# Two of three matmuls for the 64 rest rows in three down products, and five statistics in step 4

## The chip, the cores and the metric

The kernel runs on one core of a Trainium2 chip. The metric is the time of one execution on the device, in microseconds (us). Before the change three runs gave 2494.76 us as the median (2494.2 to 2495.37). A profile was taken of one further execution of the same kernel.

## The reference, cut to what matters

With x of shape [4, 1024, 1024] (batch, channel, length), the block computes

```
xn   = layernorm(x)                                   # over the last axis
s    = xn + attention over the 4 batches at each position (softmax of 4x4 scores)
gate = xn @ Wg.T ; up = xn @ Wu.T                     # Wg, Wu: 2752 x 1024, NF4 codes times scales
y    = (silu(gate) * up) @ Wd.T                       # Wd: 1024 x 2752
out  = x + s * silu(y)
```

The 2752 inner rows are 21 tiles of 128 and a rest of 64. That rest is what one half of the change is about.

## The kernel before, in words

**Numbers.** All large products run on TensorE in float16 with float32 accumulation. Each float32 operand is split in two parts, high (`hi`, the value rounded to float16) and low (`lo`, what is left). A product takes three matmuls for each 128 rows: hi·hi, hi·lo and lo·hi (`TERMS`, line 1715). The 2x2 blocks of each matrix product go through Strassen-Winograd sums, so that there are seven products instead of eight; they are called p1 to p7, and `OPERAND` gives the operand index (0 to 6) of each.

**Steps.** The gate and up products take 88 steps: two halves h of the tokens, and in each 44 pairs (u, j) of a weight tile u (0 to 21) and a token group j. In step s TensorE does four products of step s and three of step s-1, each of 12 matmuls of 128x512. VectorE (DVE) adds the results up (L1536, L1543, L1548 for p6, p7, p5; L1568, L1570 for p4, p3), multiplies gate by up (L1573, L1526), and in the same steps prepares the weights of later steps and the operands of the down products. ScalarE (ACT) decodes the NF4 codes (eight `Prelu` passes, L770), rounds to float16 (L783, L932), and applies silu (L980 on p2's sum, L990 on the other). TensorE may start p7 of step s only when VectorE has done L1568 of step s-2 (`free_bank`, semaphore `c21_made`), and p1 of step s only when ScalarE has done L980 of step s-2 (`silA_made`).

**Order on an engine.** It is written by hand. VectorE's side work of a step is put into six slots, 0 to 5, by tables (`background`, line 1470): slot 0 before L1536, 1 before L1543, 2 before L1548, 3 and 4 after it, 5 behind L1573 of the step. `STAT_AT` is such a table: it says in which step and slot the layernorm statistics (L1234, `stats`, two `bn_stats` of 128x512) of token tiles 16 to 31 are taken. Tiles 16 and up have two buffers between them, so SyncE (SP) loads tile t+2 from `in_x` (L522, `load_stat`) only when the statistics of tile t are done. SP is in order too: at step s it issues first what the step stores (L590, seven stores where the step has a job) and the scales (L566), then the loads of that step's table row. From step 8 on the statistics are used (`roots`, L1222 to L1229), and tiles 16 to 31 are normalised and transposed.

**Down products.** They come last: 28 rounds i, seven products (order p1, p6, p2, p7, p5, p4, p3) for each of four token groups tp. A round has four groups g of 11 x 3 = 33 matmuls (L1932), one group for each 128 output rows. Its operands, 2816 KB of weights from `wdsc` and 2816 KB of activations from `isc`, come by DMA into a ring of two (`load_ring`, L840 and L841, issued by ACT at the beginning of the round before). Both scratch tensors are filled from `stage` slots by `store_stage`. Row block k = 10 holds the rest: in operands 1, 2 and 3 only its partitions 64 to 127 come from real rows, since the other half is zero in both parts. After a round's group VectorE, ScalarE and GpSimd (POOL, L739) finish an output tile, and SP stores it (L703).

Of the kernel before, what the change touches and what calls it, by code (L numbers as in the profile page):

```python
# [15 lines left out]
P = 128  # L16
# [27 lines left out]
DOWN_ORDER = ["p1", "p6", "p2", "p7", "p5", "p4", "p3"]  # L44
OPERAND = {"p1": 0, "p2": 1, "p3": 2, "p4": 3, "p5": 4, "p6": 5, "p7": 6}
# [28 lines left out]
def step_of(h, u, j):  # L74
# [3 lines left out]

SPARE = [s for s in range(4, 40) if PASS[s][0] % 2]

STAT_AT = {3: {0: 16, 3: 17}, 4: {0: 18, 3: 19, 5: 20}, 5: {5: 21}, 6: {0: 22, 1: 23, 2: 24, 3: 25, 5: 26},
           7: {0: 27, 1: 28, 2: 29, 3: 30, 5: 31}}
ROOTS_AT = 8
NORM_AT = {8 + 2 * i: (16 + 2 * i, 17 + 2 * i) for i in range(8)}
XJOB_AT = {s: (2 + i // 4, i % 4) for i, s in enumerate([s for s in SPARE if s >= 24][-8:])}
# [61 lines left out]
NDOWN = 11  # L147
# [3 lines left out]
for _d in range(NDOWN):  # L151
    for _i in range(3):
        DOWN_AT[NSTEP + 3 * _d + _i] = (_d, _i)
        if _d + 1 < NDOWN:
            RAMP_AT[NSTEP + 3 * _d + _i] = (NU + _d + 1, [0, 2, 5][_i], [2, 5, 8][_i])
DOWN_OPS = [[0, 4], [5, 1, 3], [6, 2]]


STAGED = {}
# [12 lines left out]
STAGE_AT, SLOT, SLOT_USE = [], [], []  # L172
# [9 lines left out]
def slot_uses(k, last):  # L182

    return SLOT[:last + 1].count(k)
# [57 lines left out]
def build(nc, x, xt, gu_codes, d_codes, scales, out):  # L242
# [4 lines left out]
    RR = I - FT * P  # L247
    GB = H // QB
    DB = I // QB
    CH = 512  # L250
    assert RR == QB and NB == 4 and KT == 8 and FT == 21 and C == 1024

    isc = nc.dram_tensor("isc", [4, 7, P, NDOWN, 2, CH], F16, kind="Internal").ap()
    wdsc = nc.dram_tensor("wdsc", [7, P, NDOWN, 2, CH], F16, kind="Internal").ap()
# [8 lines left out]
    with ExitStack() as ctx:  # L263
# [3 lines left out]
        def sem(name):  # L267
            return ctx.enter_context(nc.semaphore(name))
# [30 lines left out]
        stage = [carve(kb, 2, F16).rearrange("p (s t) -> p s t", s=2) for kb in (210, 212, 214, 216, 168, 170, 176, 178, 180, 182)]  # L299
# [14 lines left out]
        ring_i = [carve(56 * b, 22, F16).rearrange("p (k s t) -> p k s t", k=NDOWN, s=2) for b in (0, 1)]  # L314
        ring_w = [carve(56 * b + 22, 22, F16).rearrange("p (k s g m) -> p k s g m", k=NDOWN, s=2, g=4) for b in (0, 1)]
        ring_if = [carve(56 * b, 22, F16) for b in (0, 1)]
# [31 lines left out]
        ps = ctx.enter_context(nc.psum_tensor("ps", [P, 8, 512], F32))  # L348
# [31 lines left out]
        st_out = [sem(f"st_out{i}") for i in range(NALL)]  # L380
# [7 lines left out]
        w_in = [[sem(f"w_in{b}{i}") for i in (0, 1)] for b in (0, 1)]  # L388
        xb_in = [[sem(f"xb_in{j}{o}") for o in range(7)] for j in (0, 1)]
        w4_in = sem("w4_in")  # L390
        prod = sem("prod")
        p1_copied = sem("p1_copied")
        silA_made = sem("silA_made")
# [16 lines left out]
        ri_in = [sem("ri_in0"), sem("ri_in1")]  # L410
# [94 lines left out]
        def _(sp):  # L505
# [75 lines left out]

            def store_stage(c, o):
                n = STAGED[c + (o,)]
                if c[0] == "d":
                    sp.wait_ge(d_lo, c[1] * 7 + D_ORDER.index(o) + 1)
                    dst = wdsc[o, :, c[1], :, :]
                else:
                    sp.wait_ge(c_lo, lo_count(c, o))
                    dst = isc[c[2], o, :, c[1], :, :] if c[0] == "i" else xsc[c[1] - 2, o, :, c[2], :, :]
                sp.dma_start(dst, stage[SLOT[n]]).then_inc(st_out[SLOT[n]], 16)  # L590


            sp.dma_start(s_all, scales).then_inc(scales_in, 16)
# [7 lines left out]
            for a, b in ((0, 8), (8, 16), (16, 22)):  # L601
                n = (b - a) * GB
                sp.dma_start(gsc[a:b, :, :].rearrange("t b m -> (t b) m"), st_g[0:n, a * 16:a * 16 + P]).then_inc(sc_out, 16)
            sp.wait_ge(sct_evac, 4)
            for a, b in ((0, 8), (8, 16), (16, 21)):
                n = (b - a) * GB
# [24 lines left out]
            for s in range(TOTAL):  # L631
# [31 lines left out]
                if s in DOWN_AT:  # L663
                    d, i = DOWN_AT[s]
                    for o in DOWN_OPS[i]:
                        store_stage(("d", d), o)
# [20 lines left out]
            def load_xn(tp, kt):  # L687
                n = tp * KT + kt
                if n >= 2:
                    sp.wait_ge(ms_step, 8 * (n - 1))  # L690
                else:

                    sp.wait_ge(prod, len(PRODS))
                sp.dma_start(xn_r[n % 2], xnsc[tp // 2, kt, :, :, :]).then_inc(xn_in[n % 2], 16)

            def load_xr(tp, kt, a, n):
# [8 lines left out]
            for i in range(28):  # L705
                tp, r = i // 7, i % 7
                if i and (i - 1) % 7 in (2, 4, 5, 6):
                    n, kt, a = tile_no(i - 1, 3)
# [4 lines left out]
                if r in (2, 4, 5, 6):  # L713
                    for g in range(4):
                        n, kt, a = tile_no(i, g)
                        load_xr(tp, kt, a, n)
                    for g in range(3):
                        n, kt, a = tile_no(i, g)
                        store_out(tp, kt, a, n)
            n, kt, a = tile_no(27, 3)  # L720
# [21 lines left out]
        def _(act):  # L742
# [82 lines left out]
            def load_ring(i):  # L825
                tp, r = i // 7, i % 7
                o = OPERAND[DOWN_ORDER[r]]
                b = i % 2
                if i >= 2:
                    act.wait_ge(prod2, 4 * (i - 1))  # L830
                last = max(STAGED["i", p, tp, o] for p in range(NDOWN))
                for k in range(NALL):
                    if slot_uses(k, last):
                        act.wait_ge(st_out[k], 16 * slot_uses(k, last))
                if i < 7:
                    last = max(STAGED["d", d, o] for d in range(NDOWN))
                    for k in range(NALL):
                        if slot_uses(k, last):
                            act.wait_ge(st_out[k], 16 * slot_uses(k, last))
                act.dma_start(ring_wf[b], wdsc[o, :, :, :, :].rearrange("p k s c -> p (k s c)")).then_inc(rw_in[b], 16)  # L840
                act.dma_start(ring_if[b], isc[tp, o, :, :, :, :].rearrange("p k s c -> p (k s c)")).then_inc(ri_in[b], 16)  # L841

            def reloads(s, part):

# [242 lines left out]
            for s in range(2, TOTAL + 1):  # L1087
# [76 lines left out]
                if s in GRAM_AT:  # L1164
                    k = GRAM_AT[s]
# [32 lines left out]
            for i in range(28):  # L1198
                tp, r = i // 7, i % 7
# [16 lines left out]
        def _(dve):  # L1216
# [153 lines left out]
            def slot_free(n):  # L1370

                if SLOT_USE[n]:
                    dve.wait_ge(st_out[SLOT[n]], 16 * SLOT_USE[n])
                elif SLOT[n] >= NSLOT:
                    dve.wait_ge(c_lo, JOB["x", 3, 3] * 7 + 7)

# [317 lines left out]
            for i in range(28):  # L1694
                tp, r = i // 7, i % 7
# [24 lines left out]
        def _(pe):  # L1720
            t_ = nc.tensor
            TERMS = [(0, 0), (0, 1), (1, 0)]
# [71 lines left out]
            for i, (a, n) in enumerate(((0, 128), (128, 128), (256, 96))):  # L1794
                ins = t_.transpose(ps[0:n, 4, i * P:(i + 1) * P], n_g[:, a:a + n], id32[:, :])
            ins.then_inc(sct_done, 1)
            for i, (a, n) in enumerate(((0, 128), (128, 128), (256, 80))):
                ins = t_.transpose(ps[0:n, 5, i * P:(i + 1) * P], n_u[:, a:a + n], id32[:, :])
            ins.then_inc(sct_done, 1)
            for k in range(KT):  # L1800
                ins = t_.transpose(ps[0:DB, 6 + k // 4, (k % 4) * P:(k % 4 + 1) * P], s_d[:, k, :], id32[:, :])
# [63 lines left out]
            for s in range(TOTAL + 1):  # L1865
                for i, (t, name) in enumerate(halves(s)):
# [13 lines left out]
                    bank = p6_bank(t) if name in ("p6", "r") else BANK[name] + 3 * (t % 2)  # L1880
                    first, end = name not in ("p2", "p4", "p3"), name not in ("p1", "p7", "p5")
                    if u == LAST and name == "r":
                        for k, (w, o) in enumerate(zip(REST_W, (4, 2))):
                            need(t, name, w, o)
                            ins = product(t, bank, w, o, k == 0, k == 1)
                    else:
                        w, o = (OPERAND[name],) * 2 if u != LAST else (REST_W[0], 0) if name == "p1" else (REST_W[1], 1)
                        need(t, name, w, o)
                        ins = product(t, bank, w, o, first, end)
# [5 lines left out]
            for i in range(28):  # L1895
                tp, r = i // 7, i % 7
                b = i % 2
                pe.wait_ge(rw_in[b], 16 * (i // 2) + 16)
                pe.wait_ge(ri_in[b], 16 * (i // 2) + 16)
                for g in range(4):  # L1900
                    bank = g if r in (0, 2, 4, 6) else 4 + g
                    if i == 0:

                        if g == 0:
                            pe.wait_ge(silA_made, TOTAL - 1)
                        elif g == 1:
                            pe.wait_ge(c21_made, FULL_BEFORE[TOTAL])
                        elif g == 2:
                            pe.wait_ge(c12_made, FULL_BEFORE[TOTAL])
                        else:  # L1910
                            pe.wait_ge(silA_made, TOTAL)
                            pe.wait_ge(ia_made, TOTAL)
                    elif i == 1 and g == 2:
                        pe.wait_ge(q_made, TOTAL)
                    if r == 0 and tp:
                        pe.wait_ge(c12d_made, 4 * (tp - 1) + g + 1)
                    elif r == 1 and tp:
                        pe.wait_ge(c21d_made, 4 * (tp - 1) + g + 1)
                    elif r == 2:
                        pe.wait_ge(p1d_made, 4 * tp + g + 1)  # L1920
                    elif r == 3:
                        pe.wait_ge(qd_made, 4 * tp + g + 1)
                    elif r == 4:
                        pe.wait_ge(gt_made, 16 * tp + g + 1)
                    elif r == 5:
                        pe.wait_ge(vd_made, 4 * tp + g + 1)
                    elif r == 6:
                        pe.wait_ge(c22d_made, 4 * tp + g + 1)
                    first = r in (0, 1, 3, 4)
                    for k in range(NDOWN):  # L1930
                        for wa, xa in TERMS:
                            ins = t_.matmul(ps[:, bank, :], ring_w[b][:, k, wa, g, :], ring_i[b][:, k, xa, :],  # L1932
                                            start=first and (k, wa, xa) == (0, 0, 0),
                                            stop=r not in (0, 3, 4) and (k, wa, xa) == (NDOWN - 1, 1, 0), skip_group_check=True)
                    ins.then_inc(prod2, 1)
# [41 lines left out]
```

## Time and profile before

| | us |
|---|---|
| median of three runs | 2494.76 |
| the profiled execution | 2495.52 |
| its span, first to last instruction | 2493.7 |
| TensorE (PE) busy | 2410.8 |
| VectorE (DVE) busy | 1604.2 |
| ScalarE (ACT) busy | 1006.5 |
| GpSimd (POOL) busy | 83.5 |
| mean granted TensorE clock | 0.987 of full |

The profile gives busy time by engine, groups of instructions by source line, waits with what ended them, and the chain of work that ended last. A matmul's duration in it contains the modelled time in the pipeline, so the spacing of matmuls is read from a stretch of many: the stretch divided by their number.

### The profile page before, as it was taken

The page shows a single profiled execution, that of the slowest core. Times are in us where ns is not written, and L with a number is a line of the kernel's source. Part 1 is how long each engine was busy: PE and PEld are TensorE (multiplying, and loading weights), DVE is VectorE, ACT ScalarE, POOL GpSimd, SP SyncE. Part 2 cuts the span into 40 slices and gives each one's busy share as a digit, 9 for nine tenths or more (in the row PEclk, how much of TensorE's full clock was granted, in tenths as well). Part 3 has the DMA queues.
Part 4 walks back from the last instruction along what each step waited for, and adds up shares of the span by engine and source line. Part 5 has one row for each costly group of instructions (what it writes and reads, how often), then busy time and mean ns, then how long its engine had stood idle before and what let it go on. Part 6 is the DMA issues. An engine that isn't in the chain of part 4 may idle for free.

```text
span 2493.7 us, 30200 instructions
## 1 busy us (share of the span) xinstructions
PE 2410.8 (97%) x11214; PEld 1108.4 (44%) x11214; DVE 1604.2 (64%) x2746; ACT 1006.5 (40%) x1145; POOL 83.5 (3%) x72
## 2 busy tenths in 40 slices
PE   2898999999999999999999999999999999999999
PEld 2443444444444444444444444444444444444444
DVE  8888776668988877778878886665422432421431
ACT  8875787778787444443545422110010000001001
POOL 0000000000000000000000000000010011001011
PEclk7899999999999999999999999999999999999999
DMA  6856665657767795556655544248767767777764
GB/s 244 258 191 195 218 209 196 211 177 253 240 222 248 253 381 197 173 194 229 212 191 189 206 164 144 98 164 325 305 260 314 303 251 283 301 284 287 298 261 165
DMA packets 172126, 579.51 MB, mean 232 GB/s; under 512 B 17648, under 2 KB 42912, under 8 KB 154188
## 3 DMA queue, kind: packets, MB, share of 16 engines
q1 hardware_dynamic: 136716, 289.21, 34.3%
q10 hardware_dynamic: 35264, 288.37, 29.9%
q8 instruction: 89, 1.46, 0.2%
q14 instruction: 57, 0.47, 0.1%
HBM read 388.76 MB, written 188.75 MB: 232 GB/s over the span
## 4 chain that ended last, share of the span: by engine, by line
PE 88%; DVE 5%; issue 3%; ACT 2%; DMA 2%; POOL 0%; SPq 0%; POOLq 0%; ACTq 0%; DVEq 0%
PE ps L1787 55%; PE ps L1932 31%; DMA arena<-in_x 2%; ACT arena L770 1%; PE ps L1860 1%; DVE arena L1309 1%; PE ps L1741 1%; DVE arena L1398 0%; DVE arena L1240 0%; ACT arena L783 0%; DVE arena L1283 0%; DVE st L1234 0%; DMA arena<-in_gu 0%; DVE arena L1330 0%; ACT arena L932 0%
## 5 line engine op out<-in xcount | busy, mean ns | idle before, releaser
L1787 PE MATMUL ps<-arena 128*128 128x512 f16 x7152 | 1557.3, 380 | 21.1 <-DVE arena L1568 11.3
L1787 PEld LDWEIGHTS ps<-arena 128*128 128x128 f16 x7152 | 700.9, 98 | 864.8 <-DVE arena L1568 12.2
L1932 PE MATMUL ps<-arena 128*128 128x512 f16 x3696 | 797.9, 379 | 0.0
L770 ACT ACTIVATE arena<-arena,bias_t 128x2048 f32<-128x2048 f32 (+3 forms) x288 | 525.0, 1830 | 79.4 <-DMA arena<-in_dn 67.9
L1932 PEld LDWEIGHTS ps<-arena 128*128 128x128 f16 x3696 | 361.6, 98 | 436.1
L1398 DVE TENSOR_TENSOR arena<-arena 128x512 f16<-128x512 f32 x364 | 243.1, 683 | 10.0 <-ACT arena L932 8.7
L1196 ACT ACTIVATE arena<-arena,e_d 128x512 f32<-128x512 f32 x48 | 34.6, 721 | 424.3 <-DVE arena L1706 219.4
L980 ACT ACTIVATE arena<-ps,gate_back 128x512 f32<-128x512 f32 x84 | 57.2, 680 | 305.0 <-PE ps L1787 304.9
L739 POOL TENSOR_TENSOR arena<-arena 128x512 f32<-128x512 f32 x64 | 81.5, 1280 | 2396.0 <-DMA arena<-in_xt 2087.6
L1682 DVE SCALAR_TENSOR_TENSOR arena<-arena,sc 128x512 f32<-128x512 f32 x192 | 129.8, 743 | 0.0
L990 ACT ACTIVATE arena<-arena,gate_back 128x512 f32<-128x512 f32 x84 | 60.4, 719 | 171.3 <-DVE arena L1570 165.4
L1570 DVE TENSOR_TENSOR arena<-ps,arena 128x512 f32<-128x512 f32 x84 | 57.8, 688 | 90.4 <-PE ps L1787 90.4
L1691 DVE TENSOR_TENSOR arena<-arena 128x512 f32<-128x512 f32 x64 | 47.8, 747 | 102.0 <-ACT arena L1196 102.0
L932 ACT ACTIVATE arena<-arena 128x512 f16<-128x512 f32 x140 | 82.9, 620 | 41.7 <-DVE arena L1526 35.7
L1196 ACT ACTIVATE arena<-ps,e_d 128x512 f32<-128x512 f32 x16 | 11.0, 688 | 217.3 <-PE ps L1932 217.3
L1309 DVE TENSOR_TENSOR arena<-arena 128x512 f16<-128x512 f32 x147 | 95.9, 682 | 0.0
L1536 DVE TENSOR_TENSOR arena<-ps,arena 128x512 f32<-128x512 f32 x88 | 60.4, 686 | 54.9 <-PE ps L1787 50.8
L1568 DVE TENSOR_TENSOR arena<-ps,arena 128x512 f32<-128x512 f32 x84 | 57.7, 687 | 58.9 <-PE ps L1787 58.8
L1391 DVE CAST arena<-arena 128x512 f16<-128x512 f32 x224 | 91.1, 418 | 6.8 <-DMA isc<-arena 5.9
L783 ACT ACTIVATE arena<-arena 128x512 f16<-128x512 f32 x147 | 83.0, 619 | 27.8 <-DVE arena L1267 13.0
L1679 DVE TENSOR_SCALAR arena<-arena,sc 128x512 f32<-128x512 f32 x64 | 32.1, 543 | 89.5 <-DMA arena<-xnsc 89.5
L1543 DVE TENSOR_TENSOR arena<-ps,arena 128x512 f32<-128x512 f32 x84 | 57.7, 687 | 34.6 <-PE ps L1787 34.0
(108 smaller groups left out, 1160.1 us busy)
## 6 DMA issues: line engine op xcount, KB each, us to landing
isc<-arena SPq DMA_DIRECT2D x308, 256.0 KB, 2.6
arena<-wdsc ACTq DMA_DIRECT2D x28, 2816.0 KB, 10.0
arena<-isc ACTq DMA_DIRECT2D x28, 2816.0 KB, 18.1
arena<-xnsc SPq DMA_DIRECT2D x48, 1024.0 KB, 8.9
wsc<-arena ACTq DMA_DIRECT2D x21, 1792.0 KB, 6.7
arena<-in_x SPq DMA_DIRECT2D x48, 512.0 KB, 5.7
arena<-in_gu ACTq DMA_DIRECT2D x43, 512.0 KB, 4.6
wdsc<-arena SPq DMA_DIRECT2D x77, 256.0 KB, 2.1
```

What stands on the lines that cost most here:

```text
L739: g.tensor_tensor(o_sb[n % 4], o_sb[n % 4], xr[n % 4], ALU.add).then_inc(o_made, 1)
L770: a_.activation(buf, src, ACT.Prelu, bias=bias_t[:, i:i + 1], scale=scale, alpha=alpha).then_inc(ramps, 1)
L783: a_.activation(wflat[:, b, o, 0, :], src, ACT.Copy).then_inc(w_hi, 1)
L932: a_.activation(dest(c, o)[:, 0, :], operand_of(c, o), ACT.Copy).then_inc(x_hi, 1)
L990: a_.activation(q, q, ACT.Silu, scale=gate_back[:, u:u + 1]).then_inc(silB_made, 1)
L1309: v_.tensor_tensor(wflat[:, b, o, 1, :], w_source(u, o), wflat[:, b, o, 0, :], ALU.subtract).then_inc(w_lo, 1)
L1391: v_.tensor_copy(d[:, 0, :], src).then_inc(c_hi, 1)
L1398: v_.tensor_tensor(d[:, 1, :], src, d[:, 0, :], ALU.subtract).then_inc(c_lo, 1)
L1536: v_.tensor_tensor(q, ps[:, p6_bank(s), :], p1sb, ALU.add).then_inc(q_made, 1)
L1682: v_.scalar_tensor_tensor(ms[kt][a], src[:, k, :], p, ms[kt][a], ALU.mult, ALU.add).then_inc(ms_step, 1)
L1787: ins = t_.matmul(ps[:, bank, :], wreg[:, b, w, wa, k, :], xreg[:, j, o, k, xa, :], start=start and (k, wa, xa) == (0, 0, 0), stop=stop an ...
L1932: ins = t_.matmul(ps[:, bank, :], ring_w[b][:, k, wa, g, :], ring_i[b][:, k, xa, :], start=first and (k, wa, xa) == (0, 0, 0), stop=r not ...
```

## The change

Two things are changed.

The statistics: five token tiles (18 to 22) in step 4 instead of three, and four instead of five in steps 6 and 7 each. Steps 3 and 5 keep two and one.

The rest rows: for operands 1, 2 and 3 the row block k = 10 is packed. In `wdsc` the 64 rest rows (high and low part) are written twice, to partitions 0 to 63 and to 64 to 127. In `isc` the high part of x goes to partitions 0 to 63 and the low part to 64 to 127 of one 512-wide block. One matmul over 128 partitions then does hi·hi and hi·lo of the rest, and a second one over 64 partitions does lo·hi: two matmuls where there were three. Added are a semaphore for each of the three second stores, waits on it where the slot is used again and where the ring is loaded, and a wait of SP before its second `xnsc` load of the down part.

```diff
-STAT_AT = {3: {0: 16, 3: 17}, 4: {0: 18, 3: 19, 5: 20}, 5: {5: 21}, 6: {0: 22, 1: 23, 2: 24, 3: 25, 5: 26},
-           7: {0: 27, 1: 28, 2: 29, 3: 30, 5: 31}}
+STAT_AT = {3: {0: 16, 3: 17}, 4: {0: 18, 1: 19, 2: 20, 3: 21, 5: 22}, 5: {5: 23}, 6: {0: 24, 1: 25, 3: 26, 5: 27},
+           7: {0: 28, 1: 29, 3: 30, 5: 31}}
...
+PACKED = (1, 2, 3)
...
             def store_stage(c, o):
                 n = STAGED[c + (o,)]
+                src = stage[SLOT[n]]
+                last = NDOWN - 1
                 if c[0] == "d":
                     sp.wait_ge(d_lo, c[1] * 7 + D_ORDER.index(o) + 1)
                     dst = wdsc[o, :, c[1], :, :]
+                    if c[1] == last and o in PACKED:
+
+                        sp.dma_start(wdsc[o, 0:RR, last, :, :], src[RR:P]).then_inc(dup_out[o], 16)
+                        src, dst = src[RR:P], wdsc[o, RR:P, last, :, :]
                 else:
...
+                    if c[0] == "i" and c[1] == last and o in PACKED:
+
+                        src, dst = src[RR:P], isc[c[2], o, :, last, 0, :].rearrange("(s p) t -> p s t", s=2)
-                sp.dma_start(dst, stage[SLOT[n]]).then_inc(st_out[SLOT[n]], 16)
+                sp.dma_start(dst, src).then_inc(st_out[SLOT[n]], 16)
...
+                    if n == 1:
+                        for k in (4, 5):
+                            sp.wait_ge(st_out[k], 16 * SLOT.count(k))
                 sp.dma_start(xn_r[n % 2], xnsc[tp // 2, kt, :, :, :]).then_inc(xn_in[n % 2], 16)
...
+                if i < 7 and o in PACKED:
+                    act.wait_ge(dup_out[o], 16)
...
+                n = (2 * NDOWN - (1 if o in PACKED else 0)) * CH
+                act.dma_start(ring_if[b][:, 0:n], isc[tp, o, :, :, :, :].rearrange("p k s c -> p (k s c)")[:, 0:n]).then_inc(ri_in[b], 16)
...
-                        for wa, xa in TERMS:
-                            ins = t_.matmul(ps[:, bank, :], ring_w[b][:, k, wa, g, :], ring_i[b][:, k, xa, :],
+                        packed = k == NDOWN - 1 and OPERAND[DOWN_ORDER[r]] in PACKED
+                        for wa, xa in TERMS[::2] if packed else TERMS:
+
+                            end = RR if packed and wa else P
+                            ins = t_.matmul(ps[:, bank, :], ring_w[b][0:end, k, wa, g, :], ring_i[b][0:end, k, xa, :],
```

The order on VectorE in step 4, from L1526 of step 2 (the gate-up product that ends that step's work) to L1568 of step 3. BN_STATS x2 is one tile's statistics; the psum readers L1536, L1543, L1548 stand for p6, p7, p5 of step 4, and L1568, L1570 for p4, p3 of step 3. Before:

```order
L1526 SCALAR_TENSOR_TENSOR arena<-arena,up_back 128x512
L1234 BN_STATS st<-arena 128x6 x2
L1536 TENSOR_TENSOR arena<-ps,arena 128x512
L1543 TENSOR_TENSOR arena<-ps,arena 128x512
L1309 TENSOR_TENSOR arena<-arena 128x512
L1548 TENSOR_TENSOR arena<-ps,arena 128x512
L1309 TENSOR_TENSOR arena<-arena 128x512 x2
L1234 BN_STATS st<-arena 128x6 x2
L1273 TENSOR_TENSOR arena<-arena 128x512
L1568 TENSOR_TENSOR arena<-ps,arena 128x512
```

And now (L1253 is the statistics, L1558, L1565, L1570 are p6, p7, p5, L1590 is p4):

```order
L1548 SCALAR_TENSOR_TENSOR arena<-arena,up_back 128x512
L1253 BN_STATS st<-arena 128x6 x2
L1558 TENSOR_TENSOR arena<-ps,arena 128x512
L1253 BN_STATS st<-arena 128x6 x2
L1565 TENSOR_TENSOR arena<-ps,arena 128x512
L1328 TENSOR_TENSOR arena<-arena 128x512
L1253 BN_STATS st<-arena 128x6 x2
L1570 TENSOR_TENSOR arena<-ps,arena 128x512
L1328 TENSOR_TENSOR arena<-arena 128x512 x2
L1253 BN_STATS st<-arena 128x6 x2
L1292 TENSOR_TENSOR arena<-arena 128x512
L1590 TENSOR_TENSOR arena<-ps,arena 128x512
```

Two more tiles' statistics stand ahead of L1568 (now L1590) of step 3 there. In step 6 it is one less. SP's queue there, from step 4's scales to those of step 6, before:

```order
L566 DMA arena<-gsc 64x1024 x2
L566 DMA arena<-usc 64x1024 x2
L522 DMA arena<-in_x 128x1024 x3
L590 DMA isc<-arena 128x1024 x7
L522 DMA arena<-in_x 128x1024
L566 DMA arena<-gsc 64x1024 x2
L566 DMA arena<-usc 64x1024 x2
L522 DMA arena<-in_x 128x1024 x8
```

And now:

```order
L570 DMA arena<-gsc 64x1024 x2
L570 DMA arena<-usc 64x1024 x2
L526 DMA arena<-in_x 128x1024 x5
L603 DMA isc<-arena 128x1024 x7
L526 DMA arena<-in_x 128x1024
L570 DMA arena<-gsc 64x1024 x2
L570 DMA arena<-usc 64x1024 x2
L526 DMA arena<-in_x 128x1024 x6
```

Tiles 20 to 24 are loaded ahead of step 5's seven stores, where it was tiles 20 to 22.

## Rows read from the trace of the kernel before

**Rows 1.** The page, part 4: the chain that ended last, by line.

```profile
PE ps L1787 55%; PE ps L1932 31%; DMA arena<-in_x 2%; ACT arena L770 1%; PE ps L1860 1%; DVE arena L1309 1%; PE ps L1741 1%; DVE arena L1398 0%; DVE arena L1240 0%; ACT arena L783 0%; DVE arena L1283 0%; DVE st L1234 0%; DMA arena<-in_gu 0%; DVE arena L1330 0%; ACT arena L932 0%
```

**Rows 2.** Windows: us, busy of PE, PEld, DVE, ACT, POOL, clock, DMA share, GB/s.

```profile
194.70:218.30 23.60, 23.50 (x108) 10.42 (x108) 17.77 (x29) 13.35 (x11) 0.00 (x0) 1.00 0.70 215
...
226.00:228.00 2.00, 1.43 (x4) 0.58 (x5) 2.00 (x4) 0.86 (x2) 0.00 (x0) 0.50 0.81 229
...
1690.00:2488.00 798.00, 797.64 (x3696) 361.40 (x3694) 271.58 (x423) 55.72 (x81) 80.27 (x63) 1.00 0.72 283
```

**Rows 3.** Groups of instructions on PE by form.

```profile
L1932 PE MATMUL ps<-arena 128*128 128x512 f16 x3696 | 797.9, 379 | 0.0
```

**Rows 4.** Timeline of TensorE, 105 to 285 us: start, us, instructions, idle before.

```profile
160.10 32.94 PE L1787 MATMUL ps<-arena 128*128 128x512 f16 x144 [2.94 <-DVE arena L1568]
194.75 23.50 PE L1787 MATMUL ps<-arena 128*128 128x512 f16 x108 [1.71 <-ACT arena L980]
226.57 32.76 PE L1787 MATMUL ps<-arena 128*128 128x512 f16 x144 [8.33 <-DVE arena L1568]
260.63 5.35 PE L1787 MATMUL ps<-arena 128*128 128x512 f16 x24 [1.30 <-ACT arena L980]
...
277.10 0.78 PE L1741 MATMUL ps<-id,arena 128*128 128x128 f32 x4 [2.48 <-ACT arena L937]
277.68 6.92 PE L1787 MATMUL ps<-arena 128*128 128x512 f16 x24
```

**Rows 5.** Chain of waits, 142 to 282 us: start, us, what.

```profile
212.67 11.34 DMA arena<-in_x
...
226.57 14.64 PE ps L1787 x60
...
241.84 0.74 DVE arena L1573
...
276.38 0.59 ACT arena L937
```

**Rows 6.** Timeline of VectorE, step 4 to 8.

```profile
175.98 0.68 DVE L1568 TENSOR_TENSOR arena<-ps,arena 128x512 f32<-128x512 f32 x1
...
185.62 0.75 DVE L1526 SCALAR_TENSOR_TENSOR arena<-arena,up_back 128x512 f32<-128x512 f32 x1 [5.91 <-ACT arena L990]
...
207.40 1.28 DVE L1234 BATCH_NORM_STATS2 st<-arena 128x6 f32<-128x512 f32 x2
...
217.31 1.29 DVE L1234 BATCH_NORM_STATS2 st<-arena 128x6 f32<-128x512 f32 x2 [3.47 <-DMA arena<-in_x]
...
224.04 1.29 DVE L1234 BATCH_NORM_STATS2 st<-arena 128x6 f32<-128x512 f32 x2 [3.65 <-DMA arena<-in_x]
...
225.83 0.68 DVE L1568 TENSOR_TENSOR arena<-ps,arena 128x512 f32<-128x512 f32 x1
...
247.56 0.74 DVE L1526 SCALAR_TENSOR_TENSOR arena<-arena,up_back 128x512 f32<-128x512 f32 x1
```

**Rows 7.** Tile in_x, 120 to 260 us: who waited for it (us, times).

```profile
  DVE st L1234: 10.2, 4
```

**Rows 8.** Tile in_x: loads issued 170:171, 209:210, 219.5:226 (issue to landing).

```profile
DMA to landing us min/median/max: 6.9/6.9/6.9
...
DMA to landing us min/median/max: 7.6/7.6/7.6
...
DMA to landing us min/median/max: 3.6/3.6/3.6
```

**Rows 9.** Timeline of PE, 10.5 to 14.1 us.

```profile
11.48 0.85 PE L1798 MATMUL ps<-id,arena 128*128 128x128 f32 x3
12.12 1.91 PE L1801 MATMUL ps<-id,arena 128*43 128x128 f32 x8
```

**Rows 10.** Tile wdsc and line L841 (isc): landing of the ring's loads.

```profile
DMA to landing us min/median/max: 9.5/10.0/11.7
...
DMA to landing us min/median/max: 16.5/18.1/20.4
```

More of the change, by code:

```diff
@@ L390, in build @@
         w4_in = sem("w4_in")
+        dup_out = {o: sem(f"dup_out{o}") for o in PACKED}
         prod = sem("prod")
@@ L839, in load_ring @@
                             act.wait_ge(st_out[k], 16 * slot_uses(k, last))
+                if i < 7 and o in PACKED:
+                    act.wait_ge(dup_out[o], 16)
                 act.dma_start(ring_wf[b], wdsc[o, :, :, :, :].rearrange("p k s c -> p (k s c)")).then_inc(rw_in[b], 16)
-                act.dma_start(ring_if[b], isc[tp, o, :, :, :, :].rearrange("p k s c -> p (k s c)")).then_inc(ri_in[b], 16)
+                n = (2 * NDOWN - (1 if o in PACKED else 0)) * CH
+                act.dma_start(ring_if[b][:, 0:n], isc[tp, o, :, :, :, :].rearrange("p k s c -> p (k s c)")[:, 0:n]).then_inc(ri_in[b], 16)
             def reloads(s, part):
@@ L1373, in slot_free @@
                     dve.wait_ge(st_out[SLOT[n]], 16 * SLOT_USE[n])
+                    held = next(c for c, k in STAGED.items() if k < n and SLOT[k] == SLOT[n] and SLOT_USE[k] == SLOT_USE[n] - 1)
+                    if held[:2] == ("d", NDOWN - 1) and held[2] in PACKED:
+                        dve.wait_ge(dup_out[held[2]], 16)
                 elif SLOT[n] >= NSLOT:
```

## The prediction

> **What bounds the kernel now.** I read the chain of waits first. It lies on TensorE: 55% of the span on L1787 (gate and up products), 31% on L1932 (down products) [rows 1]. Then I asked of each of the two places that the change touches whether TensorE is busy throughout.
>
> In the down part it is. From 1690 to 2488 us it is busy for 797.64 of 798.00 us at full clock [rows 2], and the group has no idle time before it [rows 3]. VectorE is busy for 271.58 us there, ScalarE for 55.72. A group of 33 matmuls takes 797.9/112 = 7.12 us, so one costs 0.2159 us; the 0.379 us of the row is its modelled stay in the pipeline. Any matmul taken away here shortens the end by 0.216 us.
>
> In steps 4 to 9 it isn't. TensorE waited 2.94, 1.71, 8.33 and 1.30 us before four of its stretches, and 2.48 us before a transpose at 277.10 [rows 4]. The wait of 8.33 us is p7 of step 7 waiting for L1568 of step 5, which VectorE ran at 225.83 [rows 6]. VectorE was late because it waited for loads of x: 10.2 us in four statistics of steps 6 and 7 [rows 7], of which 3.47 and 3.65 us stand right ahead [rows 6]. The waits have a second price. The clock in 226 to 228 us is 0.50 of full, the lower of the two levels (1.2 GHz), and 1.00 in 194.70 to 218.30 [rows 2]. By the stretches: 144 matmuls should take 144 x 0.216 + 0.16 (the last one's stay beyond its spacing) = 31.3 us and took 32.94 and 32.76 behind waits of 2.94 and 8.33 us; 24 should take 5.35 and took 6.92 behind that of 2.48. Behind waits of 1.71 and 1.30 us nothing is lost (23.50 for 108, 5.35 for 24) [rows 4]. So a long wait costs some 1.6 us more.
>
> **Where the statistics act.** From 226.57 the chain is TensorE's for 14.64 us, then L1573 at 241.84, and from there only VectorE and ScalarE up to the evacuation L937 at 276.38 that releases TensorE at 277.10 [rows 5]. So what counts is how much earlier VectorE reaches L1573 of step 6 (241.84), not TensorE's own gain. I follow VectorE; a statistic of a tile adds 1.20 us (1.28 with its tail), a 512-wide operation 0.60 (0.68 with its tail) [rows 6].
>
> Step 4 now. Tile 19 moves up, tile 20 to slot 2. Its load is issued when tile 18 is done, at 170.51 as before, and took 6.9 us [rows 8], so it lands at 177.4; VectorE arrives at 173.4 and waits 4.0 us. Then L1548 and two L1309 follow, tile 21, and L1568 of step 3 runs at 182.2 instead of 175.98. Slot 5 (tile 22) ends at 185.9. VectorE had nothing to do before 185.62, where it waited 5.91 us for ScalarE [rows 6]: this idle time is the cover. It takes two statistics (2.4 us) and the 4.0 us of waiting, less the idle bits, and 0.3 us is left over as delay. TensorE pays in between: p7 of step 5 wants L1568 of step 3 and would be ready at 179.9 (160.10 + 1.66 for the clock + 7 products of 2.59), so it waits 3.0 us, to 182.9, and again loses 1.6 us of clock. Five products later it is 197.5 instead of 194.75 when step 6 begins.
>
> Step 5: same work, 0.3 us late. Tiles 23 and 24 replace 21 and 22 as loaded ones, tile 24's load is already issued in step 4.
>
> Step 6: tile 24 has no wait; tile 25 sits in slot 1 as tile 23 did and waits 2.1 us; no statistic in slot 2; tile 26 in slot 3 has the load that tile 24 had (issued at about 209.9, 7.6 us [rows 8]), lands at 217.6, wait 1.8. L1568 of step 5 runs at 219.4, 6.4 us earlier than 225.83. TensorE has done p6 of step 7 by 197.5 + 9 x 2.59 = 220.8, so its wait of 8.33 us is gone, and the clock's loss with it. Tile 27 has the load that tile 25 had: issued at 212.8, 11.34 us in the chain [rows 5], landing 224.1; VectorE comes at 222.0, wait 2.1.
>
> Step 7: tile 28 at once, tile 29 waits 1.2 (load issued at 225.4, 3.6 us [rows 8]), tiles 30 and 31 don't wait. The waits of the four statistics sum to 7.2 us instead of 10.2, two statistics (2.4 us) are gone from the two steps, and 0.35 us in which VectorE waited for TensorE before L1570 of step 6: 3.0 + 2.4 + 0.35 - 0.3 = 5.4 us. The same by places: L1573 of step 6 at 236.2, L1526 of it at 242.2 instead of 247.56 [rows 6].
>
> What is late next: p1 of step 9 waits for L980, which moves with VectorE to 255.3, while TensorE is ready at 251.9; that is a wait of 3.4 us and, as behind 2.94, a clock loss of 1.6. The transpose at 277.10 moves to 271.7; TensorE, slowed, is there at 271.0 instead of waiting 2.48 us. A wait of 0.7 us is shorter than those that cost clock, so the 1.6 us lost at 277.68 [rows 4] are won: 5.4 + 1.6 = 7.0 us. The bounds: nothing, if VectorE's 4.0 us wait in step 4 grows by some us and eats the gain; 8.33 + 1.6 = 9.9 us, if TensorE gets all of its wait back.
>
> **The rest rows.** Three of seven products, four token groups, four output groups: 48 matmuls less, 48 x 0.2159 = 10.4 us. 48 of those that remain work on 64 partitions. No row shows such a matmul; it streams the same 512 columns, and I take 0.216 us. The built program gives them a 64x128 tile of the array and everything else of the round 128x128, so the array's tile shape is changed twice in each of 48 groups, 96 times. Bounds: from below, a 64-row matmul that ran wholly beside its neighbours would be worth another 48 x 0.216 = 10.4 us; nothing excludes it, nothing speaks for it. From above, a change that lets the pipeline run empty costs what a matmul stays beyond its spacing, 0.379 - 0.216 = 0.163 us, and if the weight load (361.40/3694 = 0.098 us [rows 2]) can't run ahead either, 0.261 us. The nearest row: three matmuls of L1798 on a full tile start at 11.48, L1801's with 43 columns (a 128x64 tile) at 12.12; that is 0.213 each, the spacing within L1801 too ((1.91 - 0.42)/7) [rows 9]. The shape changed and nothing was added. I take zero.
>
> The Trainium skill speaks against it: TensorEngine Tiling (Array Packing), Tiling Modes, says that changing the tiling mode, and not only the tile, drains the TensorE. The trace shows such a change, in columns and at half clock, without that price [rows 9]; none here is in rows. By the rule the sum would come out as in the second rival below.
>
> The stores: three more DMA issues of SP for `wdsc` in the steps of block 10, with an issue each under other work, long before round 2 loads them. The waits on the second copies are done by then. SP's new wait before the second `xnsc` load holds back that load and what is queued behind it by the landing of the last stores, a few us; VectorE, idle for two thirds of the down part [rows 2], covers it, and TensorE needs VectorE's sums only a round later. The packed activations are 128 KB of 2816 less; the loads take at most 20.4 us [rows 10] of a round of 28.5, now 27.6 in a packed one, and were hidden anyway. All this: nothing.
>
> **The sum.** 10.4 + 7.0 = 17.4 us off 2495.52 us is 2478.1. The profiled execution is 0.8 us above the median of the runs, so for the median 2477.4.
>
> **The rivals.**
> 1. The statistics bring nothing. Loads that compete (6.9, 7.6, 11.34 us for what takes 3.6 alone [rows 5, 8]) may land later in step 4, where five are now asked for in a row; each us beyond 5 of wait goes straight into step 5. For it: the landing times vary threefold. Against: in step 4 the load that matters is issued at the same moment as before. Time: 2494.8 - 10.4 = 2484.4.
> 2. Changing the tile shape costs. At 0.163 us each: 96 x 0.163 = 15.6 us, 2477.4 + 15.6 = 2493.0, no change. With the weight load in the open: 96 x 0.261 = 25.1, giving 2502.5, slower than before. It decides from 17.4/96 = 0.18 us a change. For it: the trace has no partial-row matmul. Against: rows 9. The weaker form, a third of the pipeline's stay, would give 5 us, 2482.
> 3. It is better than forecast: TensorE's whole wait comes back (9.9), or the 64-row matmul overlaps in part: 2467 to 2474.
>
> **How the numbers follow.** The forecast 0.58, with a range of its own of 2474 to 2481. Rival 1 0.18. Rival 2 0.16, of it 0.06 slower, 0.05 no change, 0.05 the weak form. Rival 3 0.08. A difference under 0.2%, 5 us, can't be told from no change: faster means under 2489.8. That gives faster 0.88, same 0.06, slower 0.06. The range takes in the forecast, rival 1, the weak form and the upper part of rival 3: 2471 to 2486.
>
> **What would show it.** The down part: L1932's successor with 3648 matmuls in 787.3 us between the first and last, no idle, and 6.91 us for a packed group. If the groups of p2, p4 and p3 take over 6.95 us, the shape change costs. The statistics: a wait for `in_x` of about 4 us in step 4, a TensorE wait of about 3 us near 180 us, none near 220, one of about 3.4 near 252; the transpose that stood at 277.10 at about 270 to 272, and the down part starting at 1690 - 7 = 1683. I am wrong if the down part starts later than 1688 (statistics), or lasts longer than 790 us (rest rows).

## The result and the profile after

The changed kernel takes 2488.45 us (median of 13 runs, 2485.38 to 2490.34) against 2494.86 us (13 runs, 2494.20 to 2496.73) for the one before: a ratio of 0.9973, interval 0.9966 to 0.9980. It is faster by 6.4 us. I had forecast 17.4 us and a range that ended at 2486: the sign was right, and the size was outside. The profiled execution took 2489.7 us with a span of 2487.6.

The down part first, in windows (us, busy time of PE, weight loads, VectorE, ScalarE, GpSimd, clock, DMA share, GB/s) and by form of matmul:

```profile
1684.00:2481.60 797.60, 797.53 (x3649) 352.76 (x3647) 269.46 (x423) 55.74 (x81) 81.18 (x63) 1.00 0.71 280
```

```profile
L1957 PE MATMUL ps<-arena 128*128 128x512 f16 x3600 | 785.3, 379 | 0.0
L1957 PE MATMUL ps<-arena 64*128 64x512 f16 x48 | 18.6, 387 | 0.0
```

Set beside [rows 2, 3]: 48 matmuls fewer, still no idle time and full clock, and the same length. The part starts at 1684.20 us and VectorE reads the last sum at 2481.57, which is 797.37 us; before it was 1689.92 to 2487.68, 797.76. Of the 10.4 us that 48 matmuls are worth 0.4 arrived. The profile counts an engine that waits between two shapes as busy, since each matmul's modelled stay of 0.379 us covers the gap.

Where it is shows in the timeline of weight loads (start, us, count, idle before), in a packed round:

```profile
1747.80 0.09 PEld L1957 LDWEIGHTS ps<-arena 64*128 64x128 f16 x1 [0.42 <-issue]
1748.12 6.37 PEld L1957 LDWEIGHTS ps<-arena 128*128 128x128 f16 x31 [0.23 <-issue]
1754.92 0.09 PEld L1957 LDWEIGHTS ps<-arena 64*128 64x128 f16 x1 [0.42 <-issue]
```

and in that of matmuls, asked for four short stretches there (a stretch shows every matmul that is in flight in it, merged):

```profile
1747.28 0.59 PE L1957 MATMUL ps<-arena 128*128 128x512 f16 x2
1747.49 0.70 PE L1957 MATMUL ps<-arena 128*128 128x512 f16 x2
...
1747.81 0.39 PE L1957 MATMUL ps<-arena 64*128 64x512 f16 x1
...
1748.12 0.39 PE L1957 MATMUL ps<-arena 128*128 128x512 f16 x1
```

Full matmuls start 0.216 us apart (here 1747.28 and 1747.49). The 64-row one (1747.81) comes 0.32 us behind, the next full one (1748.12) 0.31. The group's period, from one 64-row load to the next, is 7.12 us, that of 33 matmuls, though there are only 32.

Then the statistics. TensorE's stretches in steps 3 to 9 (start, us, idle before), to be read beside [rows 4]:

```profile
160.50 18.30 PE L1809 MATMUL ps<-arena 128*128 128x512 f16 x84 [3.10 <-DVE arena L1590]
184.48 70.20 PE L1809 MATMUL ps<-arena 128*128 128x512 f16 x312 [5.67 <-DVE arena L1590]
256.59 5.35 PE L1809 MATMUL ps<-arena 128*128 128x512 f16 x24 [1.91 <-ACT arena L999]
...
273.06 0.63 PE L1763 MATMUL ps<-id,arena 128*128 128x128 f32 x4 [2.47 <-ACT arena L956]
273.52 5.34 PE L1809 MATMUL ps<-arena 128*128 128x512 f16 x24
```

The wait of 8.33 us is gone, one of 5.67 has come in step 5, and the transpose of 277.10 stands at 273.06. Behind it the clock isn't lost this time (24 matmuls in 5.34 us, before 6.92). 4.0 + 1.7 (1.6 in these 24 matmuls, 0.1 in the transposes) is the 5.7 us by which the down part starts earlier. Behind the new wait of 5.67 us the clock is lost (granted 0.50 from 184.5 to 188.5): the 312 matmuls should take 312 x 0.216 + 0.16 = 67.6 us and take 70.20. VectorE's side, beside [rows 6]:

```profile
178.96 1.28 DVE L1253 BATCH_NORM_STATS2 st<-arena 128x6 f32<-128x512 f32 x2 [5.09 <-DMA arena<-in_x]
...
183.74 0.68 DVE L1590 TENSOR_TENSOR arena<-ps,arena 128x512 f32<-128x512 f32 x1
...
213.40 1.28 DVE L1253 BATCH_NORM_STATS2 st<-arena 128x6 f32<-128x512 f32 x2 [2.17 <-DMA arena<-in_x]
...
219.25 1.29 DVE L1253 BATCH_NORM_STATS2 st<-arena 128x6 f32<-128x512 f32 x2 [1.58 <-DMA arena<-in_x]
...
225.80 1.29 DVE L1253 BATCH_NORM_STATS2 st<-arena 128x6 f32<-128x512 f32 x2 [2.21 <-DMA arena<-in_x]
...
230.63 1.29 DVE L1253 BATCH_NORM_STATS2 st<-arena 128x6 f32<-128x512 f32 x2 [1.11 <-DMA arena<-in_x]
...
237.81 0.74 DVE L1595 SCALAR_TENSOR_TENSOR arena<-arena,up_back 128x512 f32<-128x512 f32 x1
```

To be seen are the wait of 5.09 us in step 4 (forecast 4.0), the four waits of 2.17, 1.58, 2.21 and 1.11 us (forecast 2.1, 1.8, 2.1, 1.2), and L1595 of step 6 (the old L1573) at 237.81 instead of 241.84.

### The profile page after: what moved, and what is told of

The parts are those of the page before. It is cut to its first block, busy times and chain, and to the rows that moved or that the text cites. A ratio compares the mean times of both kernels' runs of the same rounds, so it can differ in the third digit from the quotient of the medians.

```text
span 2487.6 us, 30111 instructions
## 1 busy us (share of the span) xinstructions
PE 2407.6 (97%) x11166; PEld 1098.2 (44%) x11166; DVE 1602.0 (64%) x2746; ACT 1006.4 (40%) x1145; POOL 84.4 (3%) x72
## 4 chain that ended last, share of the span: by engine, by line
PE 87%; DVE 5%; issue 3%; ACT 2%; DMA 2%; POOL 0%; SPq 0%; POOLq 0%; ACTq 0%; DVEq 0%
PE ps L1809 55%; PE ps L1957 31%; DMA arena<-in_x 2%; ACT arena L786 1%; PE ps L1882 1%; DVE arena L1328 1%; PE ps L1763 1%; DVE arena L1420 0%; DVE arena L1259 0%; DVE st L1253 0%; ACT arena L799 0%; DMA arena<-in_gu 0%; DVE arena L1302 0%; DVE arena L1349 0%; ACT arena L951 0%
## 5 line engine op out<-in xcount | busy, mean ns | idle before, releaser
L1592 DVE TENSOR_TENSOR arena<-ps,arena 128x512 f32<-128x512 f32 x84 | 57.8, 688 | 90.1 <-PE ps L1809 90.1
L1558 DVE TENSOR_TENSOR arena<-ps,arena 128x512 f32<-128x512 f32 x88 | 60.4, 686 | 55.2 <-PE ps L1809 51.1
L1590 DVE TENSOR_TENSOR arena<-ps,arena 128x512 f32<-128x512 f32 x84 | 57.7, 687 | 57.2 <-PE ps L1809 57.2
L989 ACT ACTIVATE arena<-ps 128x512 f32<-128x512 f32 x88 | 52.1, 592 | 69.8 <-PE ps L1809 66.7
```

The costliest lines, as they stand in the source:

```text
L1558: v_.tensor_tensor(q, ps[:, p6_bank(s), :], p1sb, ALU.add).then_inc(q_made, 1)
```

## The experiments

The theory: TensorE pays about 0.1 us at each change of the tile shape that the built program declares for a matmul, and the weights of the new shape are loaded late; 96 changes took back the 10.4 us. The rivals: something in the packed data or in its loads; any matmul on fewer rows; a price per 64-row matmul, not per change. Ten kernels ran. Three numbers of each profile are used: when VectorE does L1595 (L1573 in the numbering before) of step 6, when the down part starts, and how long it is from there to VectorE's last reading of a sum. These three come from one execution each. A ratio is taken against the kernel before as it ran beside that experiment (medians 2494.75 to 2495.09 us).

| kernel | median us (runs) | ratio, 95% | L1595 | down starts | down lasts |
|---|---|---|---|---|---|
| before | 2494.86 (13) | | 241.84 | 1689.92 | 797.76 |
| changed | 2488.45 (13) | 0.9973 (0.9966 to 0.9980) | 237.81 | 1684.20 | 797.37 |
| all rows | 2478.48 (5) | 0.9934 (0.9921 to 0.9946) | 234.93 | 1681.89 | 787.39 |
| 96 rows | 2477.66 (4) | 0.9932 (0.9917 to 0.9947) | 234.41 | 1681.19 | 787.61 |
| statistics only | 2487.82 (7) | 0.9971 (0.9960 to 0.9981) | 234.94 | 1681.34 | 797.75 |
| pairs | 2482.83 (5) | 0.9952 (0.9940 to 0.9965) | 235.88 | 1682.28 | 792.41 |
| packing only | 2495.35 (10) | 1.0002 (0.9993 to 1.0011) | 240.86 | 1688.94 | 797.37 |
| all rows, slot 3 | 2476.71 (5) | 0.9930 (0.9917 to 0.9942) | 233.21 | 1679.61 | 787.40 |
| all rows, late slots | 2476.79 (5) | 0.9928 (0.9914 to 0.9941) | 233.90 | 1680.87 | 787.40 |
| all rows, no loads | 2474.30 (4) | 0.9919 (0.9905 to 0.9932) | 229.82 | 1677.89 | 787.40 |
| 64 columns | 2488.68 (10) | 0.9976 (0.9967 to 0.9986) | 235.72 | 1682.12 | 798.11 |
| 64 rows inside | 2489.03 (1) | | 237.00 | 1683.42 | 797.47 |

**All 128 rows in both packed matmuls.** The low part of the weights was already stored twice, so the one line that halves the rows can go; the product then also takes in low times low.

```diff
-                            end = RR if packed and wa else P
+                            end = P
```

> Changed kernel, but the second matmul of the packed block (lo times hi) works on all 128 partitions, so it adds lo times lo; still 3648 matmuls, none on a 64x128 tile. Theory A (each change of the tile shape costs about 0.1 us, 96 of them ate the 10.4 us of the 48 matmuls): a packed group takes 6.91 us instead of 7.12, the down part 787.3 us, the kernel 2488.45 - 10.4 = 2478.1. Theory B (what ate the gain lies in the packed data, the second stores and the loads, or the time is given back by a wait): groups stay at 7.12 us and the time at 2488.

2478.48 us, and the down part 787.39. The group of all matmuls (by form) is one:

```profile
L1957 PE MATMUL ps<-arena 128*128 128x512 f16 x3648 | 787.5, 379 | 0.0
```

3648 matmuls at 0.2159 us. The same data, stores, loads and waits as in the changed kernel: theory B is out.

**96 rows.**

```diff
-                            end = RR if packed and wa else P
+                            end = 96 if packed and wa else P
```

> Changed kernel, but the second matmul of the packed block works on 96 partitions (it adds a part of lo times lo). The built program gives it a 128x128 tile. Theory A (the declared tile shape is what costs): as with 128 partitions, 2478.1, spacing 0.216 us around it. Theory C (any matmul on fewer than all partitions loads its weights late): spacing 0.31 us before and behind it as now, 2488.

2477.66 us, and the down part 787.61. Theory C is out: a matmul on 96 of the 128 rows, for which the program declares the full tile, is as cheap as any. What isn't separated is the declared shape from the number of rows that leads to it: no run declares the full tile for 64 rows. Its weight loads by form have no idle time ahead of them that is out of the ordinary (5.7 us for 48, 0.12 each):

```profile
L1957 PEld LDWEIGHTS ps<-arena 96*128 96x128 f16 x48 | 4.7, 98 | 5.7
```

**Statistics only.** The kernel before with the two lines of `STAT_AT` of the change.

> The kernel before with only the new table of statistics. If the packing is worth nothing net and the statistics all of it: 2494.86 - 6.4 = 2488.5, no different from the changed kernel; down part starts near 1684 and lasts as before. Rival: the statistics bring 4 us or less and the packing the rest: 2491.

2487.82 us, ratio 0.9971 (0.9960 to 0.9981): 6.9 us less than the kernel before beside it (2494.75), all of the change's gain within its interval. TensorE's stretches in steps 7 to 9:

```profile
218.81 31.25 PE L1787 MATMUL ps<-arena 128*128 128x512 f16 x144 [0.49 <-DVE arena L1568]
253.73 7.04 PE L1787 MATMUL ps<-arena 128*128 128x512 f16 x24 [3.67 <-ACT arena L980]
...
270.20 0.63 PE L1741 MATMUL ps<-id,arena 128*128 128x128 f32 x4 [0.79 <-ACT arena L937]
270.67 4.70 PE L1787 MATMUL ps<-arena 128*128 128x512 f16 x21
```

That is the course I had forecast: no long wait near 220, one of 3.67 near 253 with a clock loss of 1.7 us behind it (7.04 for 24 matmuls), then one of 0.79 without.

**Pairs.** The order within odd output groups is reversed in packed rounds, so that two 64-row matmuls stand next to each other.

```diff
...
+                    pk = OPERAND[DOWN_ORDER[r]] in PACKED
+                    seq = [(k, wa, xa) for k in range(NDOWN) for wa, xa in (TERMS[::2] if pk and k == NDOWN - 1 else TERMS)]
+                    if pk and g % 2:
+                        seq = seq[::-1]
...
```

> Changed kernel; in packed rounds the odd output groups do their matmuls in reverse order, so that the 64-row matmul of group 0 is followed by that of group 1, and 2's by 3's. Still 48 matmuls on 64 rows, but 48 changes of shape instead of 96. Theory A (price per change): half of 10.4 us comes back, 2483.3, and the second 64-row matmul of a pair starts 0.216 us behind the first. Theory D (price per 64-row matmul): 2488.5, and 0.31 us between the two.

2482.83 us; the down part 792.41, 5.0 us longer than with all rows. 5.02/48 = 0.105 us for a change, as against (797.37 - 787.39)/96 = 0.104 us in the changed kernel. The number of 64-row matmuls is the same in both. So it is a price per change, and the theory's halving is met. Within a pair the second 64-row matmul starts 0.23 us behind the first (1745.88, 1746.11), and the next full one 0.31 us behind that. In the weight loads the pair has one idle time of 0.42 us ahead of it and one behind:

```profile
1745.88 0.11 PEld L1958 LDWEIGHTS ps<-arena 64*128 64x128 f16 x2 [0.42 <-issue]
1746.41 13.06 PEld L1958 LDWEIGHTS ps<-arena 128*128 128x128 f16 x62 [0.42 <-issue]
```

**Packing only.** The changed kernel with the old table of statistics.

> The changed kernel with the old table of statistics: only the packing with its 64-row matmul. Theory A: the 10.4 us of 48 matmuls are eaten by 96 changes of tile shape at about 0.1 us, so no difference from the kernel before, 2494.8; packed groups at 7.12 us. Rival: the packing is worth a few us alone and the statistics fewer than 6.4 in company: 2491 or less.

2495.35 us, ratio 1.0002 (0.9993 to 1.0011): no difference from the kernel before. The wait of TensorE in step 7 is 8.11 us, as before the change.

**Inside the group, and in columns.** My argument for a price of zero had been a change of shape in columns among the transposes [rows 9]. Two more kernels ask whether the shape's direction matters, and whether the price needs the end of a group, where the psum bank changes too. (`ps[:, bank, :]` is the bank that holds a group's sum.) In both, the packed block's lo times hi matmul comes ahead of its other one:

```diff
-                        for wa, xa in TERMS[::2] if packed else TERMS:
-                            end = RR if packed and wa else P
-                            ins = t_.matmul(ps[:, bank, :], ring_w[b][0:end, k, wa, g, :], ring_i[b][0:end, k, xa, :],
+                        for wa, xa in TERMS[2::-2] if packed else TERMS:
+                            end, cols = P, RR if packed and wa else P
+                            ins = t_.matmul(ps[0:cols, bank, :], ring_w[b][0:end, k, wa, g, 0:cols], ring_i[b][0:end, k, xa, :],
...
```

and for 64 rows `end, cols = RR if packed and wa else P, P`.

> Changed kernel, but the lo times hi matmul of the packed block works on all 128 partitions and on only 64 of the 128 weight columns, so 64 output rows of each group go without that term; the program gives it a 128x64 tile. It stands ahead of the block's first matmul, inside the group. It asks whether a change of shape in columns is free in this stream, as I read it from the transposes of the kernel before. If it is: 2478.5, groups of 6.91 us. If any change of shape costs 0.104 us: 2488.5 and 7.12 us.

> Changed kernel with the 64-row matmul moved one place ahead, inside the group instead of at its end, still 96 changes of shape. If the price is the change itself: packed groups stay at 7.12 us and the down part at 797.4. If it needs the move to another psum bank beside it: 6.91 to 7.0 us and under 792.

Columns: 2488.68 us, the down part 798.11, which is (798.11 - 787.39)/96 = 0.112 us a change; the weight loads are as late as with rows:

```profile
1745.50 0.11 PEld L1956 LDWEIGHTS ps<-arena 128*64 128x64 f16 x1 [0.42 <-issue]
1745.83 6.37 PEld L1956 LDWEIGHTS ps<-arena 128*128 128x128 f16 x31 [0.23 <-issue]
```

Rows inside the group: the down part 797.47, 0.105 us a change (2489.03 us, but in one run only). So a change in columns costs about what one in rows does, and the move to another bank has no part in it.

**Tile 20 one slot later.** On top of all rows.

```diff
-STAT_AT = {3: {0: 16, 3: 17}, 4: {0: 18, 1: 19, 2: 20, 3: 21, 5: 22}, 5: {5: 23}, 6: {0: 24, 1: 25, 3: 26, 5: 27},
+STAT_AT = {3: {0: 16, 3: 17}, 4: {0: 18, 1: 19, 3: 20, 4: 21, 5: 22}, 5: {5: 23}, 6: {0: 24, 1: 25, 3: 26, 5: 27},
```

> The kernel with all 128 rows in both packed matmuls (2478.5), and in step 4 tile 20's statistics in slot 3 and 21's in slot 4 instead of 2 and 3. Theory (VectorE stands idle for tile 20's load while L1570 and two L1328 wait behind it): they fill 1.8 of the 3.6 to 5 us, L1590 of step 3 comes 1.8 us earlier, TensorE's wait in step 5 shrinks by as much, and VectorE starts step 5 at its ScalarE bound; 2477 to 2478. Rival: the time in step 4 is covered anyway: 2478.5.

2476.71 us against 2478.48 for all rows; the runs overlap (2475.15 to 2479.07, and 2477.45 to 2479.40), so the time alone doesn't tell. The trace does: the wait for tile 20 is 2.10 us where it was 3.75 with all rows, and VectorE waits for ScalarE again at the beginning of step 5:

```profile
175.96 1.29 DVE L1253 BATCH_NORM_STATS2 st<-arena 128x6 f32<-128x512 f32 x2 [2.10 <-DMA arena<-in_x]
...
183.97 0.75 DVE L1548 SCALAR_TENSOR_TENSOR arena<-arena,up_back 128x512 f32<-128x512 f32 x1 [1.29 <-ACT arena L1009]
```

L1595 of step 6 is 1.7 us earlier (233.21, was 234.93); 0.7 of it was there before the new order begins (L1548 of step 2 at 167.14, was 167.87), so about 1 us is the slot's. The kernel is 18.1 us faster than the one before (0.9930, 0.9917 to 0.9942), and its median lies 11.7 us under that of the changed one.

**Later slots in steps 6 and 7 as well.** Tiles 25, 26 and 29 one slot later each; the lines of the table are now:

```diff
+STAT_AT = {3: {0: 16, 3: 17}, 4: {0: 18, 1: 19, 3: 20, 4: 21, 5: 22}, 5: {5: 23}, 6: {0: 24, 2: 25, 4: 26, 5: 27},
+           7: {0: 28, 2: 29, 3: 30, 5: 31}}
```

> As the one before, and in steps 6 and 7 tiles 25, 26 and 29 one slot later each (2, 4 and 2), so that other work fills their waits. Theory: 1.2 to 1.7 us more off VectorE's way to L1595 of step 6, which is on the chain: 2476. Rival: the landing of tile 27's load (11 us) sets the way whatever stands before it: only tile 29's 1.1 us or nothing, 2477 to 2478.5.

2476.79 us, the same as without. The waits for tiles 25 and 29 shrink to 0.81 us and to nothing, and those for 26 and 27 grow to 2.11 and 2.63 us. The landing of tile 27's load sets the way, as the rival had it, and it comes later than before: its load can be issued only when tile 25's statistics are done, which are now later, so it goes out at 212.0 us instead of 210.6 and lands 10.8 us on (before 10.5).

**No loads.** Tiles 20 to 31 aren't loaded for their statistics; those are taken of what the buffers hold, so the scales of these tokens aren't the reference's. The counts that VectorE waits for are lowered to match.

```diff
             def load_stat(tt):
                 h, n, q = tokens(tt)
+                if tt >= 20:
+                    return
...
```

> The kernel with all 128 rows in both packed matmuls, but tiles 20 to 31 are not loaded for their statistics, which read what is in the buffers instead: the same instructions without the waits for x (its scales are not those of the reference). It bounds what the statistics' loads still cost. Theory (the waits for these loads are what holds VectorE up to step 7): VectorE has no wait for in_x, TensorE none above 2 us in steps 5 to 7, and 6 us are gained: 2472.5. Rival: the gain stops at once because ScalarE or TensorE is the next bound: 2477.

2474.30 us. VectorE has no wait for x between 160 and 245 us, and reaches L1595 of step 6 at 229.82, 5.1 us ahead of all rows. The time is 4.2 us less (2474.30 against 2478.48), and the down part starts 4.0 us earlier. Between 5.1 and 4.0 lies the clock: here 24 matmuls behind a wait of 2.47 us before the transpose take 7.03 us, 1.7 more than at full clock. With all rows the clock was lost earlier, at 253.70 (8.31 us for 24), mostly in time that TensorE would have waited before that transpose; it has no wait there, and starts the transpose at 270.76, some 0.6 us later than VectorE and ScalarE would have let it (265.07 + 5.11). So the loads of x still cost about 4 us here, of which the later slot gives 1 to 2.

## Why the prediction failed, and what of it held

**The rest rows: the step that failed is the price of changing the tile shape.** I had written: "The nearest row: three matmuls of L1798 on a full tile start at 11.48, L1801's with 43 columns (a 128x64 tile) at 12.12 ... I take zero." It is 0.104 us each, 96 times, 10.0 us of a gain of 10.4. The bound above, 0.163 us, held it; the value between the bounds was ill chosen. The row was the nearest in name and not in kind: its matmuls are float32 of 128x128, and their weight loads take 0.19 to 0.23 us themselves. Their spacing of 0.213 us is that of the same kind of transposes at 40.83 to 45.36 us (20 in 4.53 us), where the granted clock is 0.51 in the mean, so almost all at the lower level; at full clock four take 0.60 us. So half clock is read from their pace; the profile's own clock for 10.80 to 14.00 us reads 1.00. A change of shape in columns, put into the float16 stream at full clock, costs 0.112 us, about as much as one in rows. The weight loads of those transposes show a difference:

```profile
11.90 1.69 PEld L1801 LDWEIGHTS ps<-id,arena 128*43 128x43 f32 x8
```

The first load of the new shape starts at 11.90 us, together with the last matmul of the old one and 0.22 us ahead of its own matmul at 12.12. In the float16 stream it starts only with its own. Why it can run ahead in the one and not in the other wasn't tried.

I gave a chance of 0.16 to there being a price; the rule that I named beside it, from the Trainium skill, TensorEngine Tiling (Array Packing), Tiling Modes, that a change of the mode and not only of the tile drains the TensorE, was right in that the change has a price. The runs put the number to it. What they show is the weight load. Among full matmuls it starts together with the matmul before its own, 0.216 us ahead:

```profile
1747.28 0.10 PEld L1957 LDWEIGHTS ps<-arena 128*128 128x128 f16 x1
```

That is the load for the matmul at 1747.49, and it starts with the matmul of 1747.28. The load of a new shape starts with its own matmul, 0.31 to 0.32 us behind the start of the one before (1747.80, 1748.12). Whether the array runs empty and the load waits for that, or the load alone is late, can't be told apart here.

With this price in place of nothing the sum is 17.4 - 10.0 = 7.4 us, 2487.4 instead of 2477.4; measured were 2488.45.

**The statistics: mechanism and sum right, single terms off.** Forecast 7.0 us; alone they bring 6.9 (ratio 0.9971), and the changed kernel, with 0.4 us from its down part, gains 6.4. The wait for tile 20 was 5.09 us in the changed kernel's profile, 3.75 with all rows and 4.23 with statistics only; I had 4.0 from a load of 6.9 us, and in the changed kernel it took 8.0. What that did: TensorE's wait in step 5 was 5.67 us there, and 2.64 and 3.12 in the other two, against 3.0 forecast. With L1595 of step 6 at 234.93 and 234.94 us the gain is 6.9 us, and 4.0 in the changed kernel; but packing only, with the old table, has it at 240.86, 1.0 earlier than the profile before. These profiles differ by a us before any change acts, so 5.9 us beside my 5.4 is the fairer comparison (the place that I gave, 236.2, was 5.6 earlier than before and didn't quite agree with the 5.4).

**The clock.** That TensorE's loss would move from the transpose to an earlier place came true in the statistics-only kernel, with the forecast waits (3.67 us for 3.4, 0.79 for 0.7). In the changed kernel's profile the 1.6 us at the transpose were won by luck: the wait there stayed, 2.47 us, and this time no clock was lost behind it. The rule that I had read from one profile, waits from 2.48 us lose clock and those to 1.71 don't, doesn't hold: see below.

**The stores, the loads, SP's wait.** Nothing was forecast for them and nothing was found: with all rows the down part is 787.39 us, 0.1 from 787.3.

**The rivals.** The second was what came, at two thirds of its first price and twice its weak form. From 0.18 us a change the kernel would have been slower than before; 0.104 left it faster, by what the statistics bring. The first, statistics that bring nothing, did not come, nor the third. The signs to look for were given rightly: a packed group over 6.95 us (it is 7.12), and a down part over 790.

## What to carry to other kernels

A matmul that is smaller than its neighbours isn't free in a stream of full ones: if it makes the program declare another tile shape, it cost here, between float16 matmuls of 512 columns at full clock, about 0.1 us on the way in and 0.1 on the way out, half such a matmul each. Fill it up instead, with useful or harmless rows, or put the small ones side by side. And where the trace doesn't show an operation, a row with the same name under another clock and with other operands is no measurement of it: stay between the bounds.

## What the runs showed of the hardware that was not expected

**The profile hides a gap between matmuls.** The changed kernel's down part reads as busy for 797.53 of 797.60 us. Only the start-to-start spacing shows the 10 us (0.32 and 0.31 us in place of 0.216, under the 0.379 us that a matmul is drawn with).

**A wait of 2.1 to 3.5 us loses the clock in one execution and not in the next.** The shortest wait with a loss is one of 2.11 us (statistics only, 84 matmuls in 19.99 us behind it), the longest without one of 3.53. Behind 3.10 us the changed kernel ran 84 matmuls in 18.30 us, full clock, and behind 2.47 us 24 in 5.34. Other executions, in timelines of TensorE; first all rows, where both waits lose:

```profile
159.42 19.99 PE L1809 MATMUL ps<-arena 128*128 128x512 f16 x84 [2.89 <-DVE arena L1590]
...
253.70 8.31 PE L1809 MATMUL ps<-arena 128*128 128x512 f16 x24 [3.67 <-ACT arena L999]
```

then pairs, where the same two places differ:

```profile
159.55 19.99 PE L1809 MATMUL ps<-arena 128*128 128x512 f16 x84 [2.64 <-DVE arena L1590]
...
254.67 5.35 PE L1809 MATMUL ps<-arena 128*128 128x512 f16 x24 [3.53 <-ACT arena L999]
```

The loss behind such a wait is 1.3 us (6.67 for 24 matmuls behind 2.95 us, 64 rows inside) to 3.0 us (8.31 - 5.35). In windows of the all-rows kernel the granted clock is 0.50, the lower level (1.2 GHz), from 253.7 to 259.7 us, and 1.00 from 254.7 to 256.7 in pairs. It may be behind the spread of the changed kernel's runs, 5.0 us from lowest to highest against 2.5 before, but the link wasn't tested, and the kernel before spread over 4.5 us itself in another 15 runs. With the landing of tile 20's load (6.5 to 8.0 us after its issue over the eleven profiles that load it) it says how far a single profile can be trusted here: to about 3 us, by my estimate from this largest loss.
